# Fused cross attention and RWKV block: the fifth mix shares a bank with the first decay product, and the passes get new orders

## The reference, cut to what matters

```python
xn = _ln(x, ln1_w, ln1_b)
sx = _token_shift(xn, state[:, i1])
xxx = jnp.tanh((xn + sx * maa_x) @ maa_w1).reshape(b, l, 5, 1, 32)
xxx = jnp.matmul(xxx, maa_w2).reshape(b, l, 5, E)
x5 = xn[:, :, None] + sx[:, :, None] * (maa_stack + xxx)
w = jnp.exp(-jnp.exp(time_decay + jnp.tanh(x5[:, :, 1] @ decay_w1) @ decay_w2))
r, k, v = x5[:, :, 3] @ Wr.T, x5[:, :, 0] @ Wk.T, x5[:, :, 2] @ Wv.T
g = jax.nn.silu(x5[:, :, 4] @ Wg.T)
# per head, over time: out = r . (u * k v + s);  s = k v + w * s
# group norm of att, x = x + att * g @ Wo.T
# xn2 = _ln(x), shift, xk, xr; x = x + sigmoid(xr @ ffn_Wr.T) * (relu(xk @ ffn_Wk.T)**2 @ ffn_Wv.T)
```

## Time and profile before

| | us |
|---|---|
| median of 3 runs (lowest, highest) | 780.33 (779.73, 785.28) |
| the profiled execution | 782.66 |
| its span, first to last instruction | 780.9 |
| busy in the span: PE, DVE, ACT, POOL | 670.8, 647.7, 367.4, 269.7 |
| mean granted clock of TensorE | 0.952 |

### The profile page before, as it was taken

One profiled execution on the slowest core, in us unless ns is written; L12 is line 12 of the kernel. 1 busy time (PEld: TensorE's weight loads), 2 busy tenths in 40 slices (PEclk: granted clock), 3 DMA queues, 4 the chain that ended last, 5 costly groups with the idle time before them and its releaser, 6 DMA issues.

```text
span 780.9 us, 9718 instructions
## 1 busy us (share of the span) xinstructions
PE 670.8 (86%) x2736; PEld 361.8 (46%) x2736; DVE 647.7 (83%) x983; ACT 367.4 (47%) x805; POOL 269.7 (35%) x192
## 2 busy tenths in 40 slices
PE   7789999979966978898988989898898988956887
PEld 5456666656422324253453435335344442514575
DVE  2499999973457799999999999999989999899623
ACT  3478888852241245346345244644615443352342
POOL 2840000000563363353626335354443633461000
PEclk9699999999998899999999999999999999997899
DMA  2611212200290443327055151514705332350000
GB/s 69 194 55 54 67 54 61 74 14 27 61 182 0 84 82 78 65 44 161 0 108 130 32 107 38 124 26 82 161 1 107 74 60 60 66 118 0 18 9 27
DMA packets 38298, 54.17 MB, mean 69 GB/s; under 512 B 4626, under 2 KB 21154, under 8 KB 38146
## 3 DMA queue, kind: packets, MB, share of 16 engines
q1 hardware_dynamic: 36866, 50.46, 28.8%
q0 software_dynamic: 1408, 3.43, 1.3%
HBM read 16.13 MB, written 4.19 MB: 26 GB/s over the span
## 4 chain that ended last, share of the span: by engine, by line
PE 29%; DVE 26%; issue 14%; ACT 3%; DMA 1%; POOL 1%; DVEq 1%; SPq 1%; POOLq 0%; ACTq 0%
DVE state L1174 13%; PE ps_a L733 6%; PE ps_a L746 4%; PE ps_a L762 4%; PE ps_c L819 4%; PE ps_c L733 3%; PE ps_a L771 2%; DVE x L1140 2%; PE ps_att L799 1%; DVE vb L1179 1%; DVE sx L1199 1%; DVE bonus L1148 1%; DVE st L1108 1%; ACT xn L1025 1%; PE ps_a L791 1%
## 5 line engine op out<-in xcount | busy, mean ns | idle before, releaser
L658 POOL TENSOR_TENSOR x<-x,xn 128x1024 f32<-128x1024 f32 x40 | 90.0, 2251 | 236.7 <-DVE x L1140 236.7
L1174 DVE TENSOR_TENSOR_SCAN state<-ps_w,state 128x512 f32<-128x512 f32 x128 | 145.8, 1201 | 9.2 <-ACT state L940 6.2
L733 PE MATMUL ps_a<-x,wsq 128*128 128x512 f32 x256 | 119.8, 610 | 11.1 <-ACT k L990 6.0
L653 POOL TENSOR_TENSOR state<-vb,k 128x2016 f32<-128x2016 f32 x24 | 114.3, 4761 | 41.9 <-ACT k L990 18.5
L1179 DVE TENSOR_TENSOR vb<-state,r 128x2048 f32<-128x2048 f32 x32 | 110.4, 3451 | 1.7
L1140 DVE SCALAR_TENSOR_TENSOR x<-ps_a,vec,sx 128x512 f32<-128x512 f32 x80 | 57.5, 745 | 42.2 <-PE ps_a L762 32.4
L733 PEld LDWEIGHTS ps_a<-x,wsq 128*128 128x128 f32 x256 | 47.9, 193 | 72.4 <-issue 55.7
L762 PE MATMUL ps_a<-mix_t,w 128*128 128x512 f32 x128 | 64.4, 618 | 14.9 <-DVE x L1140 14.9
L296 ACT ACTIVATE probs<-ps_f,negmax 128x256 f32<-128x256 f32 x128 | 58.8, 472 | 2.0 <-DVE negmax L345 1.2
L733 PE MATMUL ps_c<-zn,wsq 128*128 128x512 f32 x64 | 35.1, 699 | 17.4 <-DVE zn L1203 17.4
L345 DVE TENSOR_REDUCE negmax<-ps_f 128x2 f32<-128x512 f32 x64 | 41.2, 686 | 8.0 <-PE ps_f L218 5.6
(11 more groups left out here) (167 smaller groups left out, 1257.6 us busy)
## 6 DMA issues: line engine op xcount, KB each, us to landing
vb<-v SPq DMA_DIRECT2D x128, 256.0 KB, 5.8
x<-in_x SPq DMA_DIRECT2D x32, 128.0 KB, 2.1
c<-in_ctx SPq DMA_DIRECT2D x32, 128.0 KB, 2.1
x_chunk<-in_x SPq DMA_DIRECT2D x8, 512.0 KB, 7.4
out<-sx SPq DMA_DIRECT2D x8, 512.0 KB, 3.0
...
```

Of the source, the lines that this page charges most:

```text
L653: nc.gpsimd.tensor_tensor(st[q][:, :, :, 1:L], src[:, :, :, 0:L - 1], wide(k[p][h][:, :])[:, :, :, 0:L - 1], ALU.mult).then_inc(kv_pool, 1)
L658: nc.gpsimd.tensor_tensor(x5[j % 2][:, :, :], x5[j % 2][:, :, :], xn[:, :, 1:L1], ALU.add).then_inc(x5_ready, 1)
L733: mm = nc.tensor.matmul(bank[:, :], wsq[:, weight, c, P * o:P * o + P], src(c), start=(c == 0), stop=(c == EC - 1))
L1174: nc.vector.tensor_tensor_scan(row, w[h][:, :], row, 0.0, ALU.mult, ALU.add).then_inc(scanned, 1)
```

## The change

The fifth mix is no longer part of `a_mix`. Its two matmuls are issued in turn with the two of `a_dec1`, into the same bank at other partitions, and its tanh stands in `a_dec`. A_ORDER loses m1 and gets an order of its own for w4, r and dec1. The bodies with flags become five functions on each engine: `fill_pass`, `first_pass`, `body`, `last_pass`, `drain_pass`. For chunk 0 DVE does the additions of xn and the product (0, 0), and its first scan stands in the fill. The core of the diff:

```diff
-    A_ORDER = ["T0", "T1", "g0", "g1", "h0", "h1", "m0", "m1", "w0a", "w0b", "w1a", "w1b", "w2a", "w2b", "dec1",
-               "v0", "v1", "w3a", "w3b", "k0", "k1", "r0", "r1", "w4a", "w4b"]
+    A_ORDER = ["T0", "T1", "g0", "g1", "h0", "h1", "m0", "w0a", "w0b", "w1a", "w1b", "dec1", "w2a", "w2b", "v0",
+               "v1", "w3a", "w3b", "k0", "k1", "w4a", "w4b", "r0", "r1"]
...
             def a_dec1(n):
-                pe.wait_ge(x5_ready, n * 5 + 1)
+                pe.wait_ge(*x5_at(n, 0))
                 bank = a_bank(n, "dec1")
                 for c in range(EC):
+                    nc.tensor.matmul(bank[0:MIX, :], t["w1"][:, c, P:P + MIX], xm[:, TOK * c:TOK * c + TOK],
+                                     start=(c == 0), stop=(c == EC - 1))
                     mm = nc.tensor.matmul(bank[DEC:2 * DEC, :], t["dw1"][:, c, :], x5_half(0)(c), start=(c == 0), stop=(c == EC - 1))
                 mm.then_inc(a_done, 1)
...
             def a_dec(n):
                 act.wait_ge(a_done, a_at(n, "dec1"))
                 wait(act, dec_done, n * 2)
                 nc.scalar.activation(low_t[DEC:2 * DEC, :], ab("dec1")[DEC:2 * DEC, :], ACT.Tanh).then_inc(dec_tanh, 1)
+                nc.scalar.activation(low_t[0:MIX, :], ab("dec1")[0:MIX, :], ACT.Tanh).then_inc(dec_tanh, 1)
...
+                if j in ADD_BY_VECTOR or (isinstance(n, int) and n == 0):
+                    dve.wait_ge(mod_ready, n * 10 + 2 * j + 2)
+                    nc.vector.tensor_tensor(x5[j % 2][:, :, :], x5[j % 2][:, :, :], xn[:, :, 1:L1], ALU.add).then_inc(x5_at(n, j)[0], 1)
```

More of the change, by code:

```diff
@@ new lines, in first_pass @@
+            def first_pass(n, p):
+                q = 1 - p
+                a_w(n, 1)
+                a_xn(n + 1)
+                state_column(n, 1, 0)
+                a_gate(n, p)
+                a_tanh(n + 1)
+                a_dec(n + 1)
+                a_w(n + 1, 0)
+                a_bias(n + 2)
+                state_column(n, 1, 1)
+                a_copy(n + 1, "v", v, v_ready)
+                state_column(n + 1, 0, 0)
+                b_att(n, 0)
+                a_copy(n + 1, "k", k[q], k_ready)
+                a_copy(n + 1, "r", r[q], r_ready)
+                c_square(n, 0)
+                a_norm(n + 2)
+                b_att(n, 1)
+                c_square(n, 1)
@@ L1089, in _, with drain_pass @@
+            def drain_pass(n, p):
+                q = 1 - p
+                c_rstd(n - 1)
+                c_x1(n - 1)
+                c_norm(n - 1)
+                c_xn2(n - 1)
+                c_kk(n - 1)
+                c_rr(n - 1)
             act.wait_ge(init_done, 3)
@@ L1260, in _, with drain_pass @@
+            def drain_pass(n, p):
+                q = 1 - p
+                c_gn(n - 1, q)
+                c_x1(n - 1)
+                c_shift(n - 1)
+                c_gate_value(n - 1)
+                c_final(n - 1)
             nc.vector.memset(eps[:, 0:1], EPS).then_inc(init_done, 1)
```

488 lines of the change are left out of this document (297 added, 191 removed).

## The result

The changed kernel takes 743.89 us (median of 4, 740.43 to 745.93), the kernel before, run beside it, 780.47 us (779.73 to 785.28). The ratio is 0.9514, with a 95% interval of 0.9459 to 0.957: 4.9% faster. The forecast was 743.0.

What follows compares the result with a forecast made beforehand. DVE, 96% busy in the loop, was taken to set the pace, through its waits and exclusion with POOL. Gains of 20.6 + 14.3 + 2.4 = 37.3 us off the median of 780.33 left 743.0; range 735 to 750.

Steps and rivals of the forecast that it cites:

- loop: Six passes, chunks 1 to 6: five of 63.0 us and one of 61.5, 376.5 against 397.1, 20.6 us gained.
- fill and first pass: Chunk 0's additions and product on DVE, dec1 earlier in the first pass: together 14.3 us gained, 5.7 in the fill.
- last pass: The wait of 4.81 us goes; DVE's gating starts at 59.4 instead of 61.8: 2.4 us gained.
- The frame: Loop pass laid out from zero at the end of a_mod(4): DVE's terms take it from 66.88 to 62.0 us.
- Product (1,1): Loop: POOL's product (0, 0), earlier with the K projection, holds DVE's product: 0.8 us lost, bounds nothing or all 4.5.
- The half clock: Loop: PE waits of 1 to 2 us keep 1.2 GHz stretches in about half the passes: 63.0 us mean.
- The swap of c_final: Loop: c_final behind a_mod(4) takes 3.5 us for 4.38, gaining 0.9; the first scan's product gains 2.55.
- The fifth mix: Loop: without it the first mix is four matmuls, so DVE's wait of 1.60 us for w0a goes.
- w4: Loop: w4b issued ahead of reductions and r projection; the wait of 0.45 us and one of 0.16 go.
- The pair on PE: Fifth mix with dec1: 1.9 us saved if the matmuls overlap, nothing if not; counted as nothing either way.
- the second loop: Rival, chance 0.22: the chain through all engines decides, with late ACT and half clock; 64.9 us a pass, total 754.
- the surplus only moves: Rival, chance 0.13: POOL's products land on other two-input DVE operations, a pass stays near 66 us, total 764.

Runs made afterwards that it cites:

- final_behind: The kernel before with only c_final's two L1217 moved behind the fifth modulation, a_mod(4): 783.42 us, ratio to before 1.0031.
- pair_only: The kernel before with only the fifth mix moved into the decay's bank and its tanh behind the decay's: 794.25 us, ratio to before 1.0173.
- three_tiles: The changed kernel with dec1's 64 columns issued as two matmuls of 32: 738.19 us, ratio to before 0.9425.
- mix_back: The changed kernel with the fifth mix in the first mix again, in a bank of its own: 753.42 us, ratio to before 0.9645.
- w4_late: The changed kernel with the fifth modulation product on PE behind the r projection again, without the fill's warm(2): 758.02 us, ratio to before 0.9701.
- final_first: The changed kernel with c_final (L1339) back ahead of the fifth modulation, a_mod(4): 742.85 us, ratio to before 0.9494.
- k_early: The changed kernel with the K projection ahead of c_recept on PE and the copies of v and k earlier on ACT: 737.00 us, ratio to before 0.9423.
- combined: no_meeting with POOL's scale mended, a_w(n, 1) behind the tanh, K projection early, dec1 in two 32-column tiles, a_bias(2) ahead of a_dec(1): 728.47 us, ratio to before 0.9308.
- pool_adds: The changed kernel with chunk 0's five additions on POOL again: 744.31 us, ratio to before 0.9544.
- no_meeting: The changed kernel with POOL's product (0, 1) ahead of the addition for j = 4 and L1339 between first scan and product: 743.48 us, ratio 0.9503.

## Why the prediction was right, and where it only seemed so

The direction, and most of what each engine does in the new pass, came as forecast. The time was met too, 743.0 for 743.89, but by a sum of which three terms were off and cancelled; that it agrees to 1 us is luck. In the profiled executions:

| term | forecast | measured |
|---|---|---|
| loop | 20.6 | 26.1 |
| fill and first pass | 14.3 | 9.4 |
| last pass | 2.4 | 1.7 |
| drain | 0 | 0.1 |
| sum | 37.3 | 37.2 |

**The loop's pass.** The frame gave 62.0 us; the passes measured 61.8. Single rows came as forecast: L1339 3.26 for 3.5, the product behind the first scan 2.29, no wait for w0 or w4. Product (1,1) came 0.5 worse, 1.3 us over its free time for 0.8. POOL's product was not late: it starts 52.7 us behind the zero of the forecast's frame, for 52.8. DVE came to its own product 0.7 us sooner than forecast (55.7 for 56.4) and so waited longer. That xn2 is ready before DVE asks held, but by 0.2 us and not 1.5.

**The half clock.** The step that failed is the mean of 63.0, with "such stretches will stay in about half of the passes". PE does still wait, 1.19 us at xm and 1.20 at xk, but the granted clock of the loop is 0.99 for 0.97, and from 283.6 to the end of the loop it is the 2.4 GHz level throughout. That is 1 us a pass, and it makes up most of the 5.5 us by which the loop is ahead of its forecast.

What the forecast had wrong is which waits bring the lower level. In the loop of the kernel before, the clock falls to 1.2 GHz five times, each time behind one PE wait of 2.25 to 2.34 us (at the bonus, L791, or at xk, as at 462.71); behind the waits of 1.2 to 2.14 us it does not fall, and not behind the one of 2.33 at 629.23 either. In final_behind and pair_only it falls behind waits of 2.14 to 2.81 us, and again not behind every one. In the kernel after, the wait at the bonus is gone and the one at xk is down to 1.16 to 1.33 us, and no fall is left; nor is there one in the middle passes of three_tiles, mix_back or w4_late, whose longest waits there are 1.8 to 1.9 us. So in these traces each slow stretch had a single wait of at least 2.0 us before it, and the waits of 1 to 2 us, on which the forecast rested, had none behind them. No run changed such a wait alone, so that this is the cause is argued and not shown.

The Trainium skill (TensorE: Matmul & The Clock Gate, HAM oscillation), read as the prediction did, would have put such a stretch into every pass; the row on the loop disagrees. The kernel that this page describes has longer waits than any in these passes, so it was read too widely.

**The swap of c_final.** The prediction booked 0.9 and 2.55 us a pass to it, and 0.8 against the early K projection. The sum is about right (2.65 forecast, 2.4 measured) and the booking is wrong. Out of the changed kernel the swap can be taken back for nothing (final_first); into the old one it goes for nothing (final_behind, where 3.0 us or more of wait for w4 take its place). As I read these two runs, what the changed kernel owes its 2.4 us of shorter DVE work to is that POOL's product (0, 0) comes early enough to share its hold with the product behind the fourth scan; the swap and that are two ways to the same gain. That the K projection's place does this is shown only for one step further (k_early, 0.46 us sooner); the step in the change itself was not undone alone.

**The fifth mix.** Forecast: 1.60 us of wait gone. mix_back loses 0.9 us a pass, and pair_only shows that the move alone costs 12 us (794.25 for 781.97; 9.6 behind the attention). By its rows it needs dec1 ahead of w2. I had that order in the first pass's argument, and not in the loop's.

**w4.** Forecast: waits of 0.45 and 0.16 gone. w4_late shows 2.1 us a pass: the term was mis-sized, because the old wait was small only as long as L1217 and the slow pass covered it. The old wait of 0.45 us said nothing of how late the operation would be in a pass that is 4 us shorter.

**The pair on PE** was costed at nothing and cost nothing in the loop. Which of the two cases holds is now a row: 3.95 us, no overlap. The Trainium skill (TensorEngine Tiling (Array Packing), Key Properties) says that changing the tiling mode drains TensorE; the row agrees. Its cover is the 1.60 us that PE waits in three_tiles. In the fill there is no such cover, and there the pair costs 2 us.

**Fill and first pass.** The first scan of chunk 1 came at 277.18, for 272.2. The stage ahead ended 0.55 us late, the pair cost 2 us on a path where PE is waited for, and v's spread landed 2.36 us behind DVE. In the first pass, DVE waits 2.33 us for an ACT instruction that I had followed on PE and not on ACT, as its timeline shows:

```profile
221.37 2.26 DVE L1282 TENSOR_TENSOR state<-vb,k 128x2016 f32<-128x2016 f32 x1 [2.36 <-DMA vb<-v]
...
253.13 1.60 DVE L1238 SCALAR_TENSOR_TENSOR wyz<-wyz,bna,x_chunk 128x1024 f32<-128x1024 f32 x1 [2.33 <-ACT x_chunk L1007]
...
273.05 4.20 DVE L1300 TENSOR_TENSOR vb<-state,r 128x2048 f32<-128x2048 f32 x1
```

`a_bias(2)` stands behind `a_w(1, 0)`; in combined, which has it ahead of a_dec, the wait is gone. The product at 273.05, for which 2.3 us had been booked, is held by POOL again. And the additions on DVE, part of the 5.7 us for the fill, are worth nothing (pool_adds); what shortens the fill is in the rest of its order, which no run took apart.

**Last pass.** The wait of 4.81 us is gone, as forecast, and the pass is 0.7 us longer than forecast (60.14 for 59.4). The gating, which had no wait here before, now waits for the group norm's scale, and then meets POOL's product as it did before:

```profile
660.21 1.41 DVE L1306 SCALAR_TENSOR_TENSOR ag<-attc,gn_eh,sq 128x512 f32<-128x512 f32 x2 [3.78 <-ACT sq L1086]
661.54 5.61 DVE L1310 SCALAR_TENSOR_TENSOR ag<-ag,gn_eh,gate 128x512 f32<-128x512 f32 x2
```

**The rivals.** Something like the second loop is real and lies 0.7 us under the pass: no_meeting ran into it at 61.1. The rival had it right in kind and wrong in size: its 64.9 was 62.2 + 1.7 + 1.0, and 61.1 lies below even the bare 62.2, so neither ACT's lateness nor the half clock was there to be added, and the sum of the loop's rows was at least 1.1 too long. That the surplus only moves is what final_first shows of the swap, though not of the change as a whole.

**What the runs account for.** Of the 37.7 us behind the attention, undoing w4's place gives back 14.1 and undoing the fifth mix's move 7.2, each in the changed kernel. The swap and the additions on DVE give back nothing. The first step of the K projection, the clock, and the orders of the fill, the first and the last pass were not undone alone.
